# Flamingo gated attention and FFN on one core: seventy matmuls of ones by the identity ahead of the first gate matmul

## The reference

```python
def _layernorm(x): return (x - mean) / sqrt(var + 1e-5)          # over the 1024
# linear cross attention, 8 heads of 64
qh = softmax(Wq q, over the 64) * 64 ** -0.5                     # q = _layernorm(x)
kh = softmax(Wk k, over the 1024); vh = Wv v                     # k = v = ctx
out = Wo (kh vh^T)^T qh + bo; out = out / norm(out) * g * sqrt(128)
x = x + tanh(g_xattn) * out
# FFN with ternary weights, 1024 -> 2752 -> 1024
deq(w) = round(clip(w / (mean|w| + 1e-5), -1, 1)) * mean|w|
x = x + tanh(g_ffn) * deq(w_down) (gate * up)                    # both of _layernorm(x)
```

## Time and profile before

| what | value |
|---|---|
| median of 3 runs | 1383.82 us |
| lowest and highest | 1381.38 and 1386.99 us |
| the profiled execution's own time | 1388.0 us |
| its span, first to last instruction | 1386.2 us |
| its mean granted TensorE clock | 0.979 |

### The profile page before, as it was taken

One profiled execution on the slowest core, in us unless ns is written; L12 is line 12 of the kernel. 1 busy time (PEld: TensorE's weight loads), 2 busy tenths in 40 slices (PEclk: granted clock), 3 DMA queues, 4 the chain that ended last, 5 costly groups with the idle time before them and its releaser, 6 DMA issues. The chain is left out here.

```text
span 1386.2 us, 30208 instructions
## 1 busy us (share of the span) xinstructions
PE 1314.9 (95%) x12408; PEld 961.9 (69%) x12408; DVE 1003.7 (72%) x1343; ACT 634.1 (46%) x879; POOL 580.5 (42%) x357
## 2 busy tenths in 40 slices
PE   4787599999999899999999999999999999999999
PEld 2454387855787558876598757885598748985994
DVE  6977778878799976887688875889578866641330
ACT  4668786853544424453434533453344443320220
POOL 0249925866274472444334451346034432240120
PEclk8998799999999999999999999999999999999999
DMA  9939999896664879778777975787677895663421
GB/s 352 408 145 336 267 288 306 243 184 151 146 163 99 174 180 244 182 181 186 168 176 174 196 187 136 200 169 186 150 184 181 179 171 130 159 173 88 138 76 46
DMA packets 401417, 260.00 MB, mean 188 GB/s; under 512 B 325312, under 2 KB 342080, under 8 KB 401280
## 3 DMA queue, kind: packets, MB, share of 16 engines
q1 hardware_dynamic: 394368, 232.90, 67.3%
q10 hardware_dynamic: 6912, 25.17, 5.7%
HBM read 152.37 MB, written 25.95 MB: 129 GB/s over the span
## 5 line engine op out<-in xcount | busy, mean ns | idle before, releaser
L1118 PE MATMUL ps<-w_dn,inter_buf 128*128 128x512 fp8e4 x1376 | 307.8, 380 | 2.0 <-DVE inter_buf L1372 1.3
L1118 PEld LDWEIGHTS ps<-w_dn,inter_buf 128*128 128x128 f16 x1376 | 134.9, 99 | 157.8 <-issue 4.7
L1804 POOL TENSOR_TENSOR qs<-qs,q_stat 128x1024 f32<-128x1024 f32 x64 | 129.6, 2024 | 232.9 <-DVE q_stat L1615 232.9
L1034 PE MATMUL ps<-zT,w_gu 128*128 128x256 f16 x1664 | 191.2, 274 | 3.0 <-DVE zT L1372 2.4
L1034 PEld LDWEIGHTS ps<-zT,w_gu 128*128 128x128 fp8e4 x1664 | 163.0, 99 | 29.2 <-DVE zT L1372 2.6
L1069 PE MATMUL ps<-w_gu 128*128 128x128 f16 x2880 | 174.0, 219 | 2.7 <-DVE w_gu L1715 1.8
L1069 PEld LDWEIGHTS ps<-w_gu 128*128 128x128 fp8e4 x2880 | 165.8, 98 | 7.1 <-issue 3.1
L1860 POOL TENSOR_TENSOR w_gu<-w_gu 128x512 f32<-128x512 f32 x60 | 82.4, 1373 | 179.8 <-DVE w_gu L1715 112.6
L1069 PE MATMUL ps<-zT,w_gu 128*128 128x128 f16 x2176 | 132.6, 219 | 0.0
L1715 DVE SCALAR_TENSOR_TENSOR w_gu<-ps,w_gu 128x512 f32<-128x512 f32 x120 | 82.5, 688 | 68.0 <-PE ps L1069 67.9
L1069 PEld LDWEIGHTS ps<-zT,w_gu 128*128 128x128 fp8e4 x2176 | 125.5, 98 | 3.9
(11 more groups left out here) (195 smaller groups left out, 2588.8 us busy)
## 6 DMA issues: line engine op xcount, KB each, us to landing
w_gu<-forms SPq DMA_DIRECT2D x158, 256.0 KB, 3.0
ct_raw<-forms SPq DMA_DIRECT2D x52, 256.0 KB, 3.1
w_dn<-in_down_w SPq DMA_DIRECT2D x19, 512.0 KB, 6.0
xb<-in_x ACTq DMA_DIRECT2D x16, 512.0 KB, 6.8
x_dram<-xb SPq DMA_DIRECT2D x16, 512.0 KB, 3.9
fin<-x_dram SPq DMA_DIRECT2D x32, 256.0 KB, 2.9
out<-fin SPq DMA_DIRECT2D x32, 256.0 KB, 2.4
inter_buf<-in_up_w SPq DMA_DIRECT2D x15, 512.0 KB, 9.7
```

The lines of the kernel that those rows point to most:

```text
L1034: last = nc.tensor.matmul(ps[:, rest_bank(g, j), s * T:s * T + T], w_gu[:, w, k, :], zT[:, h, k, :], start=(k == 0 and h == 0), stop=(k == ...
L1118: mm = nc.tensor.matmul(ps[:, down_bank(g, k), :], inter_of(g, j, u % 2, b), w_dn[:, j, hf * 512:hf * 512 + 512], start=(u == 0), stop=(u ...
L1804: nc.gpsimd.tensor_tensor(v, v, q_stat[:, u % 2, 1, :].unsqueeze(2).broadcast_to([P, 2 * HEADS, DH]), ALU.mult).then_inc(q_prob, 1)
```

## The change

A step `warm` is added to TensorE's program, seventy times. Each is one float32 matmul of a 128x128 broadcast of ones by the identity into bank 1. Nobody reads the result. The first one waits for all `qsub` and all `kexp` of batches 0 and 1, the last readers of bank 1.

```diff
+WARM = 70
...
+    "warm": [357, 358, 359, 361, 364, 366, 367, 368, 370, 371, 373, 375, 376, 377, 379, 382, 384, 385, 387, 390, 391,
+        393, 394, 395, 396, 397, 401, 402, 403, 404, 405, 413, 419, 422, 424, 429, 431, 433, 434, 435, 436, 461,
+        463, 464, 465, 469, 471, 472, 474, 476, 477, 478, 480, 484, 485, 487, 488, 489, 491, 494, 502, 506, 507,
+        508, 509, 510, 514, 515, 516, 517],
...
+    of["warm"] = [(n,) for n in range(WARM)]
...
+            def warm(n):
+                if n == 0:
+                    pe.wait_ge(q_shifted, GB * PAIRS)
+                    pe.wait_ge(k_exp, GB * PAIRS)
+                nc.tensor.matmul(ps[:, 1, 0:P], ones.broadcast_to([P, P]), ident[:, :], start=True, stop=True)
+
...
-                     "gu": gu, "product": product, "down": down})
+                     "warm": warm, "gu": gu, "product": product, "down": down})
```

More of the change, by code:

```diff
@@ L109 @@
[L109 to L112, removed]
+    "ld_ctx": [1, 97, 230, 523, 763, 1104, 1164, 1416, 1658, 1987, 2166, 2411, 2588, 2833, 3010],
@@ new lines @@
+    "ld_ctxT": [19, 150],
+    "turn_c": [287, 658, 899, 1103, 1332, 1512, 1698, 1986, 2164, 2410, 2586, 2832, 3008, 3247],
[4 rows of a table added]
+    "kmax": [20, 25, 92, 110, 162, 179, 208, 220, 268, 354, 445, 501, 555, 597, 721, 745, 777, 969, 975, 994, 1127, 1137,
+        1154, 1217, 1243, 1351, 1363, 1406, 1463, 1559, 1575, 1595, 1766, 1810, 1849, 1879, 1990, 2000, 2016, 2035,
+        2176, 2220, 2270, 2298, 2414, 2419, 2441, 2457, 2598, 2642, 2692, 2720, 2836, 2841, 2863, 2879, 3020, 3064,
+        3114, 3142, 3251, 3257, 3279, 3291],
@@ L118 @@
[L118 to L133, removed]
@@ L150 @@
[L150 to L157, removed]
@@ new lines @@
+    "ctxk": [105, 152, 217, 276, 532, 646, 761, 888, 1004, 1050, 1227, 1323, 1414, 1506, 1628, 1692, 1881, 1949, 2062,
+        2136, 2285, 2347, 2484, 2558, 2707, 2769, 2906, 2980, 3129, 3190, 3325, 3380],
+    "krec": [121, 231, 524, 753, 1002, 1232, 1415, 1617, 1889, 2042, 2310, 2464, 2732, 2886, 3154, 3298],
+    "cc_hi": [161, 295, 657, 903, 1058, 1333, 1513, 1699, 1957, 2145, 2354, 2567, 2776, 2989, 3197, 3386],
+    "cc_lo": [165, 309, 661, 907, 1064, 1334, 1516, 1703, 1960, 2149, 2358, 2571, 2780, 2993, 3201, 3387],
@@ new lines @@
+    "mprod": [169, 317, 683, 921, 1069, 1358, 1567, 1711, 1963, 2156, 2368, 2578, 2790, 3000, 3213, 3393],
+    "mev": [177, 327, 691, 932, 1073, 1366, 1571, 1717, 1966, 2165, 2378, 2587, 2800, 3009, 3219, 3398],
+    "mabs": [696, 950, 1079, 1372, 1577, 1725, 1970, 2172, 2385, 2594, 2807, 3016, 3227, 3402],
+    "msum": [700, 977, 1096, 1375, 1579, 1731, 1978, 2194, 2391, 2616, 2813, 3038, 3230, 3408],
+    "mscale": [120, 123, 735, 980, 1116, 1376, 1581, 1748, 1981, 2199, 2396, 2621, 2818, 3043, 3233, 3412],
@@ new lines @@
+    "qsub": [83, 85, 133, 151, 235, 253, 318, 343, 427, 470, 572, 665, 703, 805, 848, 957, 997, 1028, 1052, 1091, 1111,
+        1201, 1268, 1303, 1318, 1449, 1482, 1528, 1619, 1678, 1746, 1778, 1830, 1863, 1929, 1942, 2063, 2106, 2130,
+        2186, 2252, 2283, 2346, 2361, 2485, 2528, 2552, 2608, 2674, 2705, 2768, 2783, 2907, 2950, 2974, 3030, 3096,
+        3127, 3189, 3204, 3317, 3375, 3415, 3456],
+    "qexp": [87, 89, 142, 156, 240, 264, 331, 351, 503, 544, 576, 670, 709, 906, 913, 962, 1001, 1030, 1054, 1095, 1117,
+        1205, 1272, 1306, 1321, 1456, 1486, 1532, 1622, 1689, 1750, 1784, 1835, 1870, 1933, 1946, 2066, 2113, 2135,
+        2191, 2258, 2291, 2349, 2366, 2488, 2535, 2557, 2613, 2680, 2713, 2771, 2788, 2910, 2957, 2979, 3035, 3102,
+        3135, 3192, 3209, 3318, 3379, 3421, 3460],
@@ new lines @@
+    "tr": [103, 130, 196, 200, 291, 303, 409, 425],
+    "e_f": [108, 135, 197, 204, 298, 312, 417, 437],
+    "qf_hi": [539, 582, 632, 773, 818, 924, 952, 1013, 1034, 1061, 1082, 1160, 1187, 1230, 1298, 1425, 1451, 1489, 1514,
+        1639, 1668, 1702, 1763, 1805, 1865, 1890, 1948, 2019, 2077, 2132, 2162, 2239, 2282, 2309, 2363, 2439, 2499,
+        2554, 2584, 2661, 2704, 2731, 2785, 2861, 2921, 2976, 3006, 3083, 3126, 3153, 3206, 3273, 3332, 3389, 3435,
+        3476],
+    "qf_lo": [546, 586, 636, 782, 824, 928, 961, 1016, 1040, 1068, 1086, 1165, 1192, 1234, 1300, 1430, 1455, 1494, 1520,
+        1642, 1674, 1706, 1773, 1813, 1869, 1903, 1953, 2021, 2081, 2137, 2170, 2245, 2287, 2311, 2371, 2443, 2503,
+        2559, 2592, 2667, 2709, 2733, 2793, 2865, 2925, 2981, 3014, 3089, 3131, 3155, 3211, 3276, 3335, 3392, 3437,
+        3479],
@@ new lines @@
+    "turn_q": [551, 593, 758, 788, 829, 933, 1000, 1020, 1045, 1071, 1144, 1170, 1199, 1238, 1404, 1435, 1466, 1498, 1608,
+        1647, 1680, 1710, 1779, 1820, 1874, 1907, 1996, 2023, 2087, 2141, 2223, 2250, 2290, 2317, 2416, 2446, 2509,
+        2563, 2645, 2672, 2712, 2739, 2838, 2868, 2931, 2985, 3067, 3094, 3134, 3161, 3254, 3280, 3341, 3396, 3441,
+        3483],
+    "outp": [180, 182, 185, 186, 241, 244, 248, 249, 334, 337, 340, 344, 444, 448, 450, 454, 746, 749, 751, 754, 814,
[6 rows of a table added]
+    "yev": [192, 256, 369, 459, 759, 827, 1005, 1044, 1146, 1200, 1405, 1467, 1611, 1681, 1777, 1853, 1998, 2041, 2224,
[3 rows of a table added]
@@ new lines @@
+    "ssg": [202, 266, 383, 479, 770, 839, 1011, 1051, 1161, 1215, 1417, 1481, 1618, 1690, 1790, 1860, 2006, 2053, 2233,
[5 rows of a table added]
+    "ld_xr": [21, 153, 378, 637, 963, 1114, 1598, 1599, 1972, 1974, 2393, 2395, 2815, 2817, 3235, 3236],
[9 rows of a table added]
+    "zt_hi": [360, 578],
+    "zt_lo": [374, 583],
+    "z_hi": [935, 1089, 1276, 1536, 1726, 1921, 2101, 2353, 2523, 2775, 2945, 3196, 3360, 3539],
+    "z_lo": [941, 1094, 1295, 1542, 1730, 1927, 2111, 2356, 2533, 2778, 2955, 3199, 3363, 3542],
+    "turn_z": [947, 1100, 1439, 1555, 1909, 1930, 2331, 2359, 2753, 2781, 3175, 3202, 3534, 3546],
[6 rows of a table added]
@@ new lines @@
+    "down": [956, 960, 970, 973, 978, 983, 999, 1010, 1015, 1019, 1024, 1027, 1031, 1043, 1056, 1062, 1067, 1072, 1075,
[10 rows of a table added]
+    "gcopy": [602, 614, 625, 635, 647, 674, 684, 702, 716, 729, 741, 765, 789, 810, 840, 854, 864, 878, 889, 919, 931,
+        940, 1122, 1149, 1166, 1178, 1189, 1211, 1228, 1250, 1264, 1273, 1292, 1302, 1311, 1328, 1338, 1353, 1362,
+        1373, 1390, 1413, 1433, 1444, 1601, 1623, 2045, 2056, 2467, 2478, 2889, 2900, 3309, 3320, 3591, 3598],
+    "gmul": [605, 619, 628, 640, 650, 679, 687, 708, 720, 734, 747, 767, 792, 816, 846, 856, 867, 882, 893, 927, 938,
+        955, 1126, 1151, 1169, 1180, 1198, 1213, 1231, 1260, 1275, 1281, 1294, 1312, 1320, 1339, 1342, 1359, 1374,
+        1395, 1396, 1421, 1442, 1468, 1606, 1629, 2047, 2057, 2469, 2479, 2891, 2901, 3310, 3326, 3592, 3599],
```

196 lines of the change are left out of this document (87 added, 109 removed), and 174 rows, old and new, of the table WHEN.

## The result

| kernel | median | runs | lowest to highest |
|---|---|---|---|
| before | 1385.4 us | 4 | 1381.4 to 1389.2 us |
| changed | 1423.9 us | 4 | 1422.5 to 1430.6 us |

The ratio is 1.028, 95% interval 1.025 to 1.031: the change costs 38 us. I had forecast 1386.7 us, and my range ended at 1396.

What follows compares the result with a forecast made beforehand. TensorE work was taken to bound everything behind the first gate matmul, waits the part ahead. +0.35 + 9.4 - 4.2 (projections already done) - 2.7 + 0 = +2.9 us on 1383.8 gave 1386.7 us; range 1377 to 1396.

Steps and rivals of the forecast that it cites:

- Instructions and their price: Seventy warm matmuls on TensorE: 140 more instructions near 0.109 us each, 15.3 us at full clock.
- The clock: At `ctxk(2,0)` and the first gate matmuls: as much half clock as now, 0 us, with -4.1 as other bound.
- the term of +0.35 us for `kT`: Ahead of `ctxk(2,0)`: slipping queues delay the second `kT` transpose, and so `ctxk(2,0)`, by 0.35 us.
- If `kT` came 6 us earlier, they would be on the path: Ahead of `ctxk(2,0)`: the 9.80 us wait for `kT` covers the warm matmuls; 6 us earlier it would not.
- The first gate matmul: Behind `zt(1,0)`: the reordered chain of DVE and ACT steps starts it near 182.5 instead of 173.10, +9.4 us.
- said to hide under `kf_lo(2,2)`: Ahead of the gate: POOL's reorder, `x2a(1,1)` behind one more `wquant`, hides under `kf_lo(2,2)`.
- `mmx`: At `msum(3,0)` and the `down` behind it: waits of 2.09 and 0.6 us vanish, -2.7 us (bounds 0 and -2.7).
- The other waits of the earlier trace I leave: TensorE's remaining listed waits after 170 us, apart from `mmx`: left out of the sum.
- worth 2 us either way: Shuffled steps around the `zT`/`eT` waits of batches 6 and 7: could be worth 2 us either way.
- The last rival: `mmx` wait stays or moves, DVE's longer queue starves gate matmuls: +2.7 and 2 to 5 us more; chance 0.20.
- another rival: Ahead of `R(1,0)`: warm matmuls run at half clock, about +11 us, 1394.8 us; chance 0.12.

Runs made afterwards that it cites:

- run 2: Seventy warm matmuls kept, new order only up to `zt(1,0)`, old order behind it, against the kernel before: 1390.3 us, ratio 1.0025.
- run 12: Kernel before, without warm matmuls, with `ld_ctx(4,0)` moved behind `kf_hi(2,2)` on ACT's queue: 1386.4 us, ratio 0.9992.

## Why the prediction was wrong

- *Instructions and their price: right.* 140 instructions, 0.112 us each where 0.109 was taken; the warm matmuls lie in pauses, and run 2 prices them, with the new order up to `zt(1,0)`, at +0.25%.
- *The clock: a forecast that missed, at no consequence.* `ctxk(2,0)` was to stay at half clock; its 24 matmuls took 2.6 us, from 160.64 to 163.25, at full. The cause is that `kT` came in 6.8 us, most likely since `ld_ctx(4,0)` slipped from 154.66 to 157.96 (run 12 shows that without this load it takes 6.7); the term of +0.35 us for `kT` was in truth -3.7. "If `kT` came 6 us earlier, they would be on the path" was the right question; it came 3.7 us earlier and the matmuls just fitted. The Trainium skill (TensorE: Matmul & The Clock Gate, Part 4: PE-mode transpose) says of transposes that they do not count as busy for the clock. That the warm matmuls, which are plain ones, hold it now has its row: with them the clock is 1.00 from 140 to 160 us. No run has transposes in their place, so how much of that is their kind and how much the filled pauses is not told apart.
- *The first gate matmul: right within 2 us, in part by luck.* 182.5 forecast, 184.60 measured; `qt(2,2)` at 174.88 for 175.5, `zt(1,0)` at 180.29 for 179.2. The chain of DVE and ACT steps was named correctly from the earlier trace rows, but its start was not. `kf_hi(2,2)` ran at 161.23 and not at 164.3, which alone would have brought all of it 3 us sooner. In its place came the reorder of `x2m(1,1)` on DVE and `x2a(1,1)` on POOL, said to hide under `kf_lo(2,2)`: `x2a(1,1)` ended at 162.40 instead of 159.43 and held `ln2` of batch 1 on DVE, and behind it `kf_lo(2,2)` and `z(1,0)`; and `kf_lo(2,2)` took 2.39 us instead of 1.27. The two errors nearly cancel.
- *`mmx`: wrong in its worth.* The wait of 2.1 us is gone, but the 2.7 us were not won. The projection `qt` at 290 us now waits 2.20 us for `m`, and `down(0,0,0)` 6.25: 5.7 us more idle time at this place than before, where 2.7 less had been entered.
- *The step that failed:* "The other waits of the earlier trace rows I leave", with steps around the `zT` and `eT` waits "worth 2 us either way". They were put at nothing without being worked out. Of the 23.3 us more idle time behind the gate 5.7 belong to the term of `mmx` above; the other 17.6 lie in what was left out, above all the 10.06 us for `zT`, the 7.73 for `eT` and the 5.25 for `inter_buf`, less the short waits that the kernel before had there. I had walked the new order through only as far as the gate, and took for the rest that waits absent before stay absent. But TensorE's list was dense behind the gate because each store, load and transpose was issued in time; with 250 steps of its own list and 130 of SP's at other places each of them had to be walked through as well. The last rival had the direction ("costs more than it gives back", by the `mmx` wait and a longer DVE queue) at 2 to 5 us; the idle time alone was over four times its upper end and came mostly through DMA queues, which it did not name. So the range, which ended at the price of another rival, was too narrow.
- *Could it be seen in the trace of before?* Half of it. The store's place could: SP's lists of both orders show `st_x2(2,0)` going behind two transposes, which took 4.80 and 2.87 us in the changed kernel. The slow transposes had one trace only, the `kT` of the earlier trace rows, which landed after 11.2 us beside a `cx_raw` load. I counted that as the price of that transpose, and never asked why it was more than twice that of others.

What stays open: why an overlap is harmless in most places. In the changed kernel a transpose issued at 237.52 with a context load 1.0 us behind it took 7.1 us, and one at 477.57 with a load 1.5 us behind it was not slowed; and in the kernel before the `zT` transpose above took 4.6 us with a load 1.8 us behind it. The slow ones have distances of 0.7 to 1.9 us, so the distance of issue does not decide. For `zT` the packets below tell more: before, the load's packets began when the transpose's were nearly through, in the changed kernel they ran among them. For the `kT` of the earlier trace rows it is less clear, as over two thirds of its packets were through when the load's began. Nor is the load the only cause. With the new order behind the gate the `kT` transposes issued near 205 and near 222 us take 9.3 to 17.7 us in all nine profiles, with no context load beside them (one of `q_raw` follows the first by 4.8 us), where the old order has 4.3 to 8.7. TensorE did not wait for them, and what slows them is open. That the warm matmuls cost the changed kernel 11 us through the `eT` wait rests on one profile of each kernel.

## What to carry to other kernels

A table of positions that is planned anew is a change to every queue. Walk each queue through to the end, the DMA queues first, and ask of each store and transpose what it has slipped behind, before the arithmetic that the change is named after. Where a transfer takes over twice as long as its like in the same trace, find its neighbour on the other queue: it is a trap that the next change of timing may spring elsewhere. And padding a pause to hold the clock pays only if what follows it is not waiting for something else: here the clock was held, and `zt(1,0)` waited for DVE.
